# Expert gates spread over the partitions by transfers through HBM, and applied after all experts, in a fused attention and mixture-of-experts layer

## What is computed

```python
expert_scores = x_flat @ router_w.T
top_scores, selected = jax.lax.top_k(expert_scores, TOPK)      # TOPK = 2
top_scores = softmax(top_scores)
...
h = jax.nn.silu(x1) * x3                # x1 = x @ w1[e], x3 = x @ w3[e], 128 wide
routed = ragged_dot(h, w2b, gs)         # h @ w2[e], 512 wide
weighted = routed * scores_sorted[:, None]
out_flat = zeros.at[scatter_indices].add(weighted)
```

## Time and profile before

| | us |
|---|---|
| median of 3 runs | 1225.65 (1221.99 to 1226.95) |
| the profiled execution | 1230.7 |
| its span in the trace | 1228.6 |
| PE busy | 1111.8 (90% of the span) |
| DVE busy | 892.7 (73%) |
| ACT busy | 712.2 (58%) |
| POOL busy | 163.9 (13%) |

### The profile page before, as it was taken

One profiled execution on the slowest core, in us unless ns is written; L12 is line 12 of the kernel. 1 busy time (PEld: TensorE's weight loads), 2 busy tenths in 40 slices (PEclk: granted clock), 3 DMA queues, 4 the chain that ended last, 5 costly groups with the idle time before them and its releaser, 6 DMA issues.

```text
span 1228.6 us, 18308 instructions
## 1 busy us (share of the span) xinstructions
PE 1111.8 (90%) x6080; PEld 528.5 (43%) x6080; DVE 892.7 (73%) x1095; ACT 712.2 (58%) x828; POOL 163.9 (13%) x153
## 2 busy tenths in 40 slices
PE   5389999998999999998988998999899999999886
PEld 4137433743335543333732743374333454333252
DVE  3155688768887589888576668866888767988756
ACT  4253468336884477886336347833688446788611
POOL 4220121102001011001004003110200101100000
PEclk9689999999999999998999999999899999999978
DMA  9901540163001450001064163016300145000000
GB/s 215 223 23 45 128 104 1 35 138 103 2 1 36 105 137 1 2 1 35 10 131 106 36 137 104 2 35 138 103 2 1 36 90 117 1 2 1 2 1 35
DMA packets 65680, 74.41 MB, mean 61 GB/s; under 512 B 14224, under 2 KB 48016, under 8 KB 65552
## 3 DMA queue, kind: packets, MB, share of 16 engines
q1 hardware_dynamic: 49968, 58.74, 18.9%
q0 software_dynamic: 13584, 11.54, 6.2%
q10 hardware_dynamic: 2000, 2.51, 0.7%
HBM read 25.58 MB, written 8.39 MB: 28 GB/s over the span
## 4 chain that ended last, share of the span: by engine, by line
PE 70%; DVE 18%; issue 6%; SPq 2%; ACT 1%; DMA 1%; POOL 1%; DVEq 1%; ACTq 0%; POOLq 0%
PE sc L1053 18%; PE bank L1075 15%; PE sc L943 10%; DVE psum_k L743 10%; PE sc L1192 7%; PE bank L943 7%; PE sc L1093 4%; PE bank L1093 2%; PE sc L1207 2%; SPq L364 2%; DVE stats L819 2%; DVE res L816 1%; PE sc L1138 1%; PE bank L1200 1%; DVE res L826 1%
## 5 line engine op out<-in xcount | busy, mean ns | idle before, releaser
L577 ACT ACTIVATE prob<-sc 128x1024 f32<-128x1024 f32 x544 | 525.5, 1025 | 168.9 <-PE sc L1053 158.3
L743 DVE TENSOR_TENSOR psum_k<-psum_k,prob 128x2048 f32<-128x2048 f32 x170 | 395.7, 2327 | 5.9 <-ACT prob L577 0.8
L1053 PE MATMUL sc<-q_st,k_st 128*128 128x512 f32 x1088 | 332.7, 426 | 30.5 <-DMA q_st<-q_lo 21.9
L1053 PEld LDWEIGHTS sc<-q_st,k_st 128*128 128x128 f32 x1088 | 185.4, 190 | 277.8 <-ACT prob L577 175.1
L1075 PE MATMUL bank<-prob,v_sb 128*32 128x512 f32 x2176 | 288.6, 606 | 0.0
L467 POOL TENSOR_SCALAR_AFFINE_SELECT prob<-prob 128x1024 f32<-128x1024 f32 x64 | 86.5, 1388 | 618.6 <-ACT prob L577 618.4
L1192 PE MATMUL sc<-prob,w_sb 128*128 128x512 bf16 x512 | 122.7, 383 | 2.9 <-DVE prob L892 2.9
L743 DVE TENSOR_TENSOR psum_k<-prob 128x2048 f32<-128x2048 f32 x28 | 64.1, 2289 | 69.3 <-ACT prob L577 65.3
L1075 PEld LDWEIGHTS bank<-prob,v_sb 128*32 128x32 f32 x2176 | 43.7, 108 | 106.5 <-issue 91.6
L943 PE MATMUL bank<-q_st,wq_hi 128*128 128x512 f32 x240 | 81.0, 402 | 0.0
L609 ACT ACTIVATE prob<-sc 128x512 f32<-128x512 f32 x64 | 37.3, 597 | 68.1 <-PE sc L1192 68.0
(11 more groups left out here) (127 smaller groups left out, 1019.1 us busy)
## 6 DMA issues: line engine op xcount, KB each, us to landing
q_st<-q_hi SPq DMA_DIRECT2D x128, 128.0 KB, 2.7
q_st<-q_lo SPq DMA_DIRECT2D x128, 128.0 KB, 2.8
res<-in_x SPq DMA_DIRECT2D x8, 1024.0 KB, 5.3
res<-ob_sb POOLq DMA_DIRECT2D x8, 1024.0 KB, 10.2
out_x<-res SPq DMA_DIRECT2D x32, 256.0 KB, 5.7
res<-in_xT SPq DMA_DIRECT2D x7, 1024.0 KB, 5.2
w_sb<-in_w POOLq DMA_DIRECT2D x8, 256.0 KB, 14.2
prob<-in_wqkvT ACTq DMA_DIRECT2D x4, 288.0 KB, 6.0
```

What stands on the lines that cost most here:

```text
L577: nc.scalar.activation(prob[t % NP][:, half * HW:(half + 1) * HW], score_half(q // TB, 2 * t + half).rearrange("p m n -> p (m n)"), ACT.Ex ...
L743: nc.vector.tensor_tensor(acc[:, :], first[:, :], prob[t % NP][:, :], ALU.add).then_inc(add_v, 1)
L1053: last = nc.tensor.matmul(dst, k_st[:, k * P:(k + 1) * P], q_st[slot][:, c * HJ:(c + 1) * HJ, at:at + P], start=True, stop=not shift)
```

## The change

The gates no longer go through PE to the partitions. DVE ends its chain at `gate` (no split in two parts); PE turns it (4 transposes, 8 rows instead of 16); ACT copies the 8 rows to `gT`, starts a transfer of them to `gate_hbm` (16 KB in HBM), and after the silu of expert 4 waits for that transfer and starts 8 transfers of 256 KB, each of which reads one expert's row 128 times, once for each partition, into `gate_row[e]` in SBUF. Only then come the silus of experts 5 to 7. DVE computes all 8 products first, in place in `silu[e]`, and then all 8 `hT`. PE runs the 8 `up` one behind another, with no gate matmuls, and all 32 down matmuls now stand behind the first score tile of the next block.

```diff
-        silu = [prob[1][:, i * BT:(i + 1) * BT] for i in range(4)]
-        prod = [prob[2][:, i * BT:(i + 1) * BT] for i in range(4)]
+        silu = [prob[1 + e // 4][:, (e % 4) * BT:(e % 4 + 1) * BT] for e in range(E)]
+        gate_row = [prob[(4, 0)[e // 4]][:, (e % 4) * BT:(e % 4 + 1) * BT] for e in range(E)]
+        gate_hbm = nc.dram_tensor("gate_hbm", (2, E, BT), F32, kind="Internal").ap()
...
                     for e in range(E):
                         act.wait_ge(up_done, count(b, up_done, E * g + e + 1))
-                        if e >= 4:
-                            act.wait_ge(prod_done, count(b, prod_done, E * g + e - 3))
-                        nc.scalar.activation(silu[e % 4], LOW[2 * (e % 3)], ACT.Silu).then_inc(silu_done, 1)
+                        nc.scalar.activation(silu[e], LOW[2 * (e % 3)], ACT.Silu).then_inc(silu_done, 1)
                         if e == 2:
                             act.wait_ge(gates_turned, count(b, gates_turned, g + 1))
-                            nc.scalar.activation(gT[0:2 * E, :], top[0][0:2 * E, :], ACT.Copy).then_inc(gT_ready, 1)
+                            nc.scalar.activation(gT[:, :], top[0][0:E, :], ACT.Copy).then_inc(gT_ready, 1)
+                            act.wait_ge(gT_ready, count(b, gT_ready, g + 1))
+                            act.wait_ge(part_done, count(b, part_done, g + 1))
+                            act.dma_start(gate_hbm[g % 2], gT[:, :]).then_inc(gate_out, 16)
+                        if e == 4:
+                            act.wait_ge(gate_out, count(b, gate_out, 16 * (g + 1)))
+                            for i in range(E):
+                                act.dma_start(gate_row[i], gate_hbm[g % 2, i:i + 1, :].broadcast_to([P, BT])).then_inc(gate_in[i], 16)
...
-                    for e in range(3):
+                    for e in range(E):
                         times_linear(g, e)
-                    for e in range(E):
-                        if e == 0 or 3 <= e + 1 < E and e > 2:
-                            times_linear(g, max(e + 1, 3))
-                        dve.wait_ge(prod_done, count(b, prod_done, E * g + e + 1))
-                        dve.wait_ge(gate_done, count(b, gate_done, E * g + e + 1))
-                        nc.vector.tensor_tensor(hT[:, e, :], gate_bank(e)[:, :], prod[e % 4], ALU.mult).then_inc(h_done, 1)
                         if e == 3:
                             with if_more(dve, b, g):
                                 judge(b, g + 1)
+                    for e in range(E):
+                        dve.wait_ge(prod_done, count(b, prod_done, E * g + e + 1))
+                        dve.wait_ge(gate_in[e], count(b, gate_in[e], 16 * (g + 1)))
+                        nc.vector.tensor_tensor(hT[:, e, :], gate_row[e], silu[e], ALU.mult).then_inc(h_done, 1)
...
-                def gate_rows(g, e):
-
-                    if e >= 2:
-                        pe.wait_ge(h_done, count(b, h_done, E * g + e - 1))
-                    nc.tensor.matmul(gate_bank(e)[:, :], pick[:, e:e + 1].broadcast_to([P, P]), gT[:, :], start=True, stop=True).then_inc(gate_done, 1)
-
...
-                    for e in range(2):
-                        gate_rows(g, e)
-                    for e in range(4, E):
-                        up(g, e)
-                        gate_rows(g, e - 2)
-                    gate_rows(g, E - 2)
-                    pe.wait_ge(prod_done, count(b, prod_done, E * g + 6))
-                    down(g, 0, EARLY)
-                    gate_rows(g, E - 1)
-                    down(g, 1, EARLY)
+                    pe.wait_ge(gT_ready, count(b, gT_ready, g + 1))
```

More of the change, by code:

```diff
@@ L56 @@
 BOUND_KV = 1e9
-EARLY, LATE = range(5), range(5, E)
 TILES = [(q, k) for q in range(NQ) for k in [q] + list(range(q))]
@@ L267, in build @@
         up_done = sem("up_done")
-        gate_done = sem("gate_done")
+        gate_out = sem("gate_out")
+        gate_in = [sem(f"gate_in{e}") for e in range(E)]
         silu_done = sem("silu_done")
@@ L1194, in up, with down @@
                     last.then_inc(up_done, 1)
-                def gate_rows(g, e):
-                    if e >= 2:
-                        pe.wait_ge(h_done, count(b, h_done, E * g + e - 1))
-                    nc.tensor.matmul(gate_bank(e)[:, :], pick[:, e:e + 1].broadcast_to([P, P]), gT[:, :], start=True, stop=True).then_inc(gate_done, 1)
-                def down(g, t, experts):
-                    for e in experts:
+                def down(g, t):
+                    for e in range(E):
                         if t == 0:
@@ L1208, in down @@
                                                 start=(e == 0), stop=(e == E - 1))
-                    if experts[-1] == E - 1:
-                        last.then_inc(down_done, 1)
+                    last.then_inc(down_done, 1)
                 def experts(g):
@@ L1218, in experts @@
                         up(g, e)
-                    pe.wait_ge(ghl_ready, count(b, ghl_ready, g + 1))
+                    pe.wait_ge(gate_ready, count(b, gate_ready, g + 1))
                     for t in range(TB):
-                        last = nc.tensor.transpose(top[0][0:2 * E, t * P:(t + 1) * P], ghl[:, t, :], ident[:, :])
+                        last = nc.tensor.transpose(top[0][0:E, t * P:(t + 1) * P], gate[:, t, :], ident[:, :])
                     last.then_inc(gates_turned, 1)
-                    up(g, 3)
-                    pe.wait_ge(gT_ready, count(b, gT_ready, g + 1))
+                    for e in range(3, E):
+                        up(g, e)
                     with if_more(pe, b, g):
@@ L1248, in _ @@
                 finish_experts(NG - 1)
-V_STEPS = NG * (2 * TB + 11)
+V_STEPS = NG * (2 * TB + 9)
 def max_steps(g):
```

38 lines of the change are left out of this document (8 added, 30 removed).

## The result

The changed kernel takes 1274.6 us (median of 4 runs, 1267.15 to 1277.02), the kernel before beside it on the same chip 1226.3 (4 runs): a ratio of **1.0386 (95% interval 1.0332 to 1.044)**. It is slower, as forecast, but by 47 us (by the ratio) to 48 (by the medians) where 22.5 were forecast: 1274.6 lies above the range of 1232 to 1268. The profiled execution of the changed kernel was the fastest of its four (1267.15, span 1265.4).

The account below looks back on a forecast made before the run. It took the passages out of the experts to hang on when a tile's last down matmul, which needs `hT`, is there for DVE. Later statistics 11.8 plus clock 10.7 made 22.5 us on 1225.65: 1248 us, range 1232 to 1268.

Parts of the forecast that it names:

- Up to the last `up`: Passage out of the experts: without the gates' split the first product starts some 0.65 us sooner; last `up` ends 137.6, before 139.5.
- Starting the transfers: On ACT behind expert 4's silu: eight starts at 0.52 us each, 4.2 in all, with silus of experts 5 to 7 behind.
- The rows of gates: Where SP stacks: transfers served in turn, eight pairs at 1.24 us take 9.9; last row lands 144.7, last `hT` 145.4.
- Rival (b): Seven passages: stacking transfers go first, rows of gates land late, 3.5 us each, with the clock falling: 1273 us; chance 0.15.
- From `hT` to the statistics: Behind the last `hT`: 24 down matmuls 5.2 us, issue 0.55, one tile's statistics 1.66; 1.0 us later in six middle passages.
- The clock: PE's granted clock falls after its pause: 1.7 us lost, taken as 11 of 14 for each of 8 passages, 10.7 us.

Follow-up runs that it names:

- e2: Changed kernel, with the second half of SP's stacking transfers held until the last row of gates has landed (also written e2_stack_waits): 1237.0 us, ratio 1.0077.
- e1_no_rows: Changed kernel without the transfer to HBM and the eight back; multiplications take a tile already in SBUF, so gates are not applied: 1222.2 us, ratio 0.9971.
- e5_jump_late: Changed kernel, with the last residual and second normalisation put inside both branches of DVE's guard, so its jump comes behind them: 1275.2 us, ratio 1.0377.
- the filling: Changed kernel plus unused PE matmuls, 16 behind the last `up` and 5 between down matmuls of tile 0: 1281.6 us, ratio 1.0452.
- e9: Changed kernel with gates as bf16 in scratch and rows, and the second half of SP's stacking held until the last row landed: 1224.6 us, ratio 0.9958.
- e7: Changed kernel with the second half of SP's stacking held until the last row landed, and DVE's jump moved behind the normalisation: 1238.8 us, ratio 1.008.
- e8: Changed kernel with gates as bf16 in the scratch and rows, 1 KB pieces instead of 2, as many packets: 1257.4 us, ratio 1.0233.
- e6: Kernel before, with all 32 down matmuls behind the next block's first scores and DVE's jump moved behind the normalisation: 1238.2 us, ratio 1.0065.

## Why the prediction was too low

**Up to the last `up`: right.** P0 comes 0.5 us sooner against the statistics before it (21.48 against 21.98; 0.65 forecast), the `up`s follow one another, and none waits.

**Starting the transfers: right in kind, a little short.** 0.52 each was taken; where SP does not stack it is 0.49, and in e2 0.47; beside the stacking it is 4.7 to 5.9 us for the eight, 5.71 in the first passage, 0.71 each. The last product is at P0 + 11.1 to 12.3 (10.3 at the end of the kernel) where 11.0 was forecast. It costs nothing, since the rows are later.

**The rows of gates: the term that was sized too small, and most of the miss.** The mechanism was right: both queues take turns (922 and 923 packets, above), and the last row sets the last `hT` where SP stacks. But I costed a row at 0.68 us of full engines from a stretch of large transfers, and a transfer of the stacking at 0.56. By packets it is (122 + 64) ns for a turn of both queues, 146 packets a row on 16 engines: 146 x 186 / 16 = 1.70 us a row at most, where 1.24 was taken; 1.51 was measured, and the first row landed at P0 + 8.1, where the sum would have 7.3. The last `hT` came 2.8 us later than forecast in the middle passages and 4.2 later at the second sequence: 6 x 2.8 + 4.2 = 21 us, of the 27 by which the statistics of all eight passages missed the forecast. Rival (b) had this at 3.5 us each, for another reason (the stacking first), which the even spacing of the landings speaks against. At the end of the kernel, with no stacking, DVE's serial work set it, as forecast, 0.75 us sooner than the sum had it.

**From `hT` to the statistics: the step whose mechanism was wrong.** It was forecast at 7.6 us, with PE's down matmuls and "0.55 of issue", and it took 10.0 in the middle passages. What I had read in the earlier trace rows as PE's work and 0.55 of issue was DVE's jump: in the kernel before, it runs from 142.3 to 145.37, and PE's scores and the late matmuls of tiles 0 and 1 (to 144.83) lie inside it. Its branches there:

```profile
L780 DVEq COMPARE_BRANCH  x2: 47/54/61, 141.9 to 142.3; - x2
```

I took the chain's word for it, and then moved the last `hT` in the sum without the jump that stands behind it. In the changed kernel the first residual comes 3.0 to 3.75 us behind the last `hT` in the middle passages, and 0.70 where there is no jump. Over the forecast with its clock term in it (7.6 + 1.34) that is 1.1 us in each of six passages, 6 to 7 us. The passage to the second sequence, which has no jump, showed 7.4 us against 9.7 in the first passage before the change; that difference was in front of me and asked for a reason.

That the 7.6 lies near those 7.4 is luck. At the full clock the 7.4 are 0.74 to the first residual and then DVE's own four residuals and statistics, 6.67 us, one behind another; the sum had 24 down matmuls and one tile of DVE's in their place.

**The clock: it fell as forecast, and in the middle passages the jump hid what it costs.** Where no jump stands between the last `hT` and the statistics, the length of this stretch follows the time that PE spends at the lower clock inside it:

| passage | at the lower clock, us | last `hT` to statistics, us |
|---|---|---|
| second sequence, kernel before | 0 | 7.41 |
| end, changed kernel | 2.35 | 8.53 |
| second sequence, e1_no_rows | 3.00 | 8.85 |
| middle passages, e5_jump_late (mean) | 3.34 | 9.08 |
| second sequence, e2_stack_waits | 3.70 | 9.19 |
| second sequence, changed kernel | 5.15 | 9.91 |

It is 7.4 us and half of that time, within 0.2 us, in all 34 passages of this kind in the traces (those without the filling). Two of them in the stretch view (as above):

```profile
634.57:641.98 7.41, 4.81 (x23) 1.96 (x20) 5.92 (x12) 1.28 (x1) 0.00 (x0) 1.00 0.09 17
653.13:663.04 9.91, 8.07 (x25) 2.93 (x25) 6.24 (x12) 0.00 (x0) 0.00 (x0) 0.74 0.01 4
```

The first is the kernel before, the second the changed one. So the clock cost 2.5 us at the second sequence and 1.1 at the end, where 1.34 each was forecast. In the six middle passages it costs next to nothing: DVE stands in its jump anyway, and from the first residual on it takes 6.64 us in four of them and 6.98 in two, against 6.65 before. Some 4 of the 10.7 us forecast are there. But this is not a low price of the clock: with the jump moved away (e5) it is 1.7 us in each middle passage. Jump and lower clock run side by side, and the longer one counts. That the clock term was in the sum hid some of what was missing for the jump.

**Behind the passages.** The prediction took the attention as unchanged; it is 4.9 us shorter, and the time at the lower clock in it is 27 us instead of 41, which at half speed would be 6.8. Put together against P0, in the middle passages 3.0 us were forecast with the clock in it, and 6.9 came: rows + 2.8, jump and clock together + 1.1.

What stays open: why the adds of the attention keep PE waiting less in the kernel before with all down matmuls last (the gain of 0.9 to 1.2%; PE's waits for them are 7.1 and 7.2 us there, and 7.2 in e1 and e9 too, but 13 to 18 in the changed kernel, e2, e5, e7 and e8, which have that order as well), and what makes the second packet of instructions in e6 late.

## What to carry to other kernels

A row spread over 128 partitions was 128 packets here: cost it by packets of its size in a stretch in which the other queue is loaded, in turns, and start it where no bulk transfer runs, or hold that one back. When two passages with the same work differ (9.7 and 7.4 us here), find the instruction that only one of them has, register work and branches too, before using either in a sum; a releaser named by the profile may be only the last that the profile can see. Two delays that run side by side, as the jump and the lower clock here, are not to be added, and taking away one shows the other. And a stall that is moved along an engine's serial work is not removed: it pays only where the engine has queued work to hide it.

## What the chip showed that I had not expected

- A taken branch of DVE over a long piece of program costs 2.8 to 3.6 us until the next instruction, with an 8 KB packet of an instruction queue about 1 us behind it; it cost nothing when DVE still had work queued (4.5 us from branch to residual in e9, with none of it idle for the jump). A wait for a late row right ahead of it took that cover away (e2, e9).
- Packets of 2 KB took 97 ns alone and 136 ns beside the 1 KB packets of the other queue (71 ns); packets of 1 KB took 70 ns in their place. The two queues moved equal numbers of packets, not of bytes (922 and 923).
- Starting eight transfers took ScalarE's queue 3.9 us at the end of the changed kernel and mostly 3.7 in e2, when SyncE started none, and 4.7 to 5.9 beside it.
- Between the last `hT` and the statistics each microsecond at TensorE's lower clock cost half a microsecond, in 34 passages, wherever the jump did not cover it.
